# Two-stage graph network on one core: bank fills dropped, the second stage started from the message block over the cast masks, mask conversion moved ahead of the tile steps

## The reference, cut to what matters

```
h = relu(layernorm(x))                                        # setup
Wh = h @ W;  e = leaky_relu(Wh@a1 + (Wh@a2).T, 0.2)
att = softmax(where(adj > 0, e, -9e15), axis=-1)
x = x + relu(att @ Wh)                                        # first stage, attention
h = relu(layernorm(x))                                        # per tile of 128 rows
node = h @ W1                                                 # 16 columns
m = einsum('nk,nkf->nf', node, einsum('nc,kcf->nkf', h, W2))  # the "messages"
x = x + relu(adj @ m + node @ b)                              # second stage, gather
```

## Time and profile before

| | |
|---|---|
| median of 3 runs | 1854.64 us (1854.27 to 1855.09) |
| profiled execution | 1854.6 us, its span 1852.9 us |
| busy: PE / PEld | 1820.1 us (98%) / 1582.7 us (85%) |
| busy: DVE / ACT / POOL | 1206.4 (65%) / 1328.4 (72%) / 702.5 us (38%) |
| first stage, matmuls L812 | 8192 records, 979.2 us busy |
| second stage, matmuls L856 | 2048 records, 558.5 us busy |
| mean granted TensorE clock | 0.996 |

### The profile page before, as it was taken

How to read it: one execution, slowest core, us unless ns; L and a number is a source line. 1 busy time by engine, 2 the same in 40 slices (tenths; PEclk the granted TensorE clock), 3 DMA queues, 4 the chain that set the end, 5 groups by cost and what they waited for, 6 DMA issues and landing times.

```text
span 1852.9 us, 38382 instructions
## 1 busy us (share of the span) xinstructions
PE 1820.1 (98%) x13364; PEld 1582.7 (85%) x13364; DVE 1206.4 (65%) x1519; ACT 1328.4 (72%) x2145; POOL 702.5 (38%) x524
## 2 busy tenths in 40 slices
PE   8899999999999999999999999999999999999998
PEld 5799989888988988898888889888777788888886
DVE  7566667777776777777677777767655543443434
ACT  5866788778778878887887788788455655555554
POOL 0000256655655665565556556555544400000000
PEclk9999999999999999999999999999999999999999
DMA  9788876776777677767767776772843344345330
GB/s 297 294 332 319 321 285 242 297 289 265 265 301 285 243 293 291 269 259 301 287 245 294 286 275 253 295 288 110 357 154 145 145 159 182 136 174 207 149 150 23
DMA packets 105811, 452.23 MB, mean 244 GB/s; under 512 B 6736, under 2 KB 15136, under 8 KB 87968
## 3 DMA queue, kind: packets, MB, share of 16 engines
q1 hardware_dynamic: 86720, 356.53, 51.7%
q10 hardware_dynamic: 12208, 75.62, 10.0%
q0 software_dynamic: 6832, 19.41, 2.8%
HBM read 364.46 MB, written 87.07 MB: 244 GB/s over the span
## 4 chain that ended last, share of the span: by engine, by line
PE 91%; DVE 4%; ACT 2%; issue 2%; DMA 0%; DVEq 0%; SPq 0%; ACTq 0%
PE ot_ps L812 47%; PE mt_ps L856 13%; PE ot_ps L856 13%; PE hw_ps L776 11%; PE mt_ps L746 6%; PE h_ps L771 1%; DVE p_sb L903 1%; ACT wh_mask L497 1%; DVE att L960 1%; DVE p_sb L888 1%; ACT prod L574 1%; DVE p_sb L984 1%; DMA wh_mask<-in_x_dram 0%; DVE keep L965 0%; PE h_ps L783 0%
## 5 line engine op out<-in xcount | busy, mean ns | idle before, releaser
L812 PE MATMUL ot_ps<-wh_mask,p_sb 128*128 (+1 forms) x8192 | 979.2, 277 | 4.9 <-DVE p_sb L984 4.9
L812 PEld LDWEIGHTS ot_ps<-wh_mask,p_sb 128*128 128x128 f32 x8192 | 941.1, 192 | 6.6 <-issue 5.9
L984 DVE SCALAR_TENSOR_TENSOR p_sb<-zb,qcol,mt 128x1024 f32<-128x1024 uint8 (+1 forms) x512 | 770.9, 1535 | 266.7 <-ACT mt L509 213.4
L379 POOL TENSOR_TENSOR prod<-prod 128x1024 f32<-128x1024 f32 (+2 forms) x192 | 413.0, 2151 | 515.4 <-ACT prod L574 499.0
L497 ACT ACTIVATE wh_mask<-adj_sb 128x2048 uint8<-128x2048 f32 x256 | 492.6, 1928 | 1.1 <-ACT mt L509 1.1
L638 ACT ACTIVATE mask<-adj_sb 128x1024 fp32r<-128x1024 uint8 x240 | 255.3, 1065 | 176.3 <-PE ot_ps L856 176.3
L509 ACT ACTIVATE mt<-mt_ps 128x1024 uint16<-128x1024 uint16 x256 | 267.7, 1046 | 144.4 <-PE mt_ps L746 142.4
L1024 DVE CAST mask<-adj_sb 128x1024 fp32r<-128x1024 uint8 x272 | 201.9, 749 | 250.1 <-PE mt_ps L856 248.2
L574 ACT ACTIVATE prod<-hw_ps,node 128x128 f32<-128x128 f32 x1024 | 278.8, 385 | 92.1 <-PE hw_ps L776 92.1
L856 PE MATMUL mt_ps<-mask,msgs 128*128 128x512 f32 x1024 | 282.9, 398 | 4.2 <-issue 3.4
L856 PE MATMUL ot_ps<-mask,msgs 128*128 128x512 f32 x1024 | 275.6, 391 | 0.9
(11 more groups left out here) (113 smaller groups left out, 582.5 us busy)
## 6 DMA issues: line engine op xcount, KB each, us to landing
adj_sb<-in_adj_dram SPq DMA_DIRECT2D x128, 2048.0 KB, 7.9
maskT_d<-mt ACTq DMA_DIRECT2D x64, 1024.0 KB, 5.2
adj_sb<-maskT_d SPq DMA_DIRECT2D x32, 2048.0 KB, 7.7
keep_d<-keep POOLq DMA_DIRECT2D x64, 128.0 KB, 5.9
p_sb<-keep_d SPq DMA_DIRECT2D x4, 2048.0 KB, 12.0
msg_d<-msg POOLq DMA_DIRECT2D x56, 128.0 KB, 5.9
msgs<-msg_d SPq DMA_DIRECT2D x7, 1024.0 KB, 8.8
wh_mask<-in_x_dram SPq DMA_DIRECT2D x8, 512.0 KB, 7.5
```

The source lines that it names most:

```text
L379: pool.tensor_tensor(prod[:, 0:n, :], prod[:, 0:n, :], prod[:, n:2 * n, :], ALU.add)\
L812: ins = pe.matmul(ot_ps[h][:, (t - t0) * ROW:(t - t0 + 1) * ROW], p_sb[:, r, t * P:(t + 1) * P], rows, start=False, stop=end and t == t1 - 1)
L984: dve.scalar_tensor_tensor(p_sb[:, r, :], zbf[:, bass.ds((ib % 2) * BLK, BLK)], qcol[:, bass.ds(tile + b_, 1)], mtb[:, p, k, :, b_], ALU.m ...
```

## The change

Four things change, all in the order of work and in waits; no tile changes its size.

1. `start_block` is gone. The first L812 matmul of each bank in a block has `start=True` (before: the zeros matmul had), and in front of it PE waits for its bank alone (`ot_copied`). The eight transposes of the turn's first step come ahead of these waits. For this PE's first turn of a block is written out ahead of its loop (`alone=True`), as DVE's was.
2. `ORDER = (5, 0, 1, 2, 3, 4, 6, 7)`: the second stage takes j block 5 first. Its messages are loaded by SP once all transposes are done, ahead of the waits for stores and L812.
3. PE waits for the last copies of the `ot_ps` banks only at the half ib = 1 of the first step, and ACT converts its half of step 0 ahead of these copies.
4. In the first pass DVE converts step t+1 at step t, ahead of the tile steps of t (before: step t, behind them).

```
-            def start_block(ib, last):
-                for h in range(3):
-                    if not (isinstance(ib, int) and ib == 0):
-                        pe.wait_ge(ot_copied, 3 * ib - 2 + h)
-                    pe.matmul(ot_ps[h][:, :], zeros16[:, :], zeros16[:, :].unsqueeze(1).to_broadcast([P, 4, P]), start=True, stop=False)
...
+                            begin = isinstance(jg, int) and jg == 0 and p == 0 and k == 0 and b_ == 0
...
                             for h, (t0, t1) in enumerate(GROUPS):
+                                if begin and finish:
+                                    pe.sem_inc(past_pe, 1)
+                                    pe.wait_ge(ot_copied, 3 * ib - 2 + h)
+                                    pe.sem_inc(past_pe, 1)
...
-                                                    p_sb[:, r, t * P:(t + 1) * P], rows, start=False, stop=end and t == t1 - 1)
+                                                    p_sb[:, r, t * P:(t + 1) * P], rows, start=begin and t == t0, stop=end and t == t1 - 1)
...
-            attention_loop(pe, turn, start_block)
+            attention_loop(pe, turn, alone=True)
```

```
+        ORDER = (5, 0, 1, 2, 3, 4, 6, 7)
...
             sp.wait_ge(turned, C * NB * NB)
+            sp.wait_ge(kept, (ORDER[0] + 1) * T + 2)
+            load_messages(0)
             for p in range(2):
                 sp.wait_ge(mt_stored[p], 16 * NB * IT)
             for r in range(4):
                 sp.wait_ge(p_used[r], 4 * NB * IT)
-            for s in range(NB - 1):
-                sp.wait_ge(kept, (s + 1) * T + 2)
+            for s in range(1, NB - 1):
+                sp.wait_ge(kept, (ORDER[s] + 1) * T + 2)
                 load_messages(s)
```

```
                         if ends_block(jg) and p == 1 and k == 3:
+                            if last:
+                                convert(0, True, 0)
                             copy_sums(ib)
...
-            for t in range(2):
-                convert(0, True, t)
+            convert(0, True, 1)
```

```
                     for ib in range(2):
+                        if t == 0 and first and ib == 1:
+                            pe.wait_ge(ot_copied, 3 * NB)
...
-            pe.wait_ge(ot_copied, 3 * NB)
             pe.wait_ge(evicted, C * NB * NB)
```

```
             for t in range(NT):
                 mi, at = t // PERIOD, t % PERIOD
+                if 2 <= t + 1 < NT:
+                    convert(0, True, t + 1)
                 if at == 1 and mi < T:
                     finish_last(mi, (2,))
                 elif at == PERIOD - 1 and mi + 1 < T:
                     finish_last(mi + 1, (0, 1))
-                if t >= 2:
-                    convert(0, True, t)
```

More of the change, by code:

```diff
@@ L306, in load_messages @@
             def load_messages(s):
-                sp.dma_start(msgs[:, s * T:(s + 1) * T, :, :].rearrange("p n c f -> p (n c f)").bitcast(FP32),
-                             msg_d[:, s * T:(s + 1) * T, :].rearrange("p n f -> p (n f)").bitcast(FP32))\
+                o = ORDER[s]
+                sp.dma_start(msgs[:, o * T:(o + 1) * T, :, :].rearrange("p n c f -> p (n c f)").bitcast(FP32),
+                             msg_d[:, o * T:(o + 1) * T, :].rearrange("p n f -> p (n f)").bitcast(FP32))\
                   .then_inc(msgs_in[s], 16)
@@ L323, in load_masks @@
                 sp.dma_start(masks_w[:, q, :, :],
-                             maskT_d[s, bass.ds(2 * ii, 2), :, :].rearrange("i p w -> p i w"))\
+                             maskT_d[ORDER[s], bass.ds(2 * ii, 2), :, :].rearrange("i p w -> p i w"))\
                   .then_inc(masks_in[q], 16)
@@ L592, in copy_sums, with convert @@
                                    ot_ps[h][:, 0:(t1 - t0) * ROW], ACT.Copy).then_inc(ot_copied, 1)
+            def convert(ii, first, t):
+                s, r = t // T, t % 2
+                for ib in range(2):
+                    if not on_dve(first, t, ib):
+                        act.wait_ge(masks_in[s % 4], 16 * (ii * (NB // 4) + s // 4 + 1))
+                        if not (first and t < 2):
+                            act.wait_ge(conv_used[r][ib], ii * (NT // 2) + t // 2)
+                        act.activation(mask32[:, r, ib, :], masks[:, s % 4, ib, t % T // 2, :, t % 2], ACT.Copy)\
+                           .then_inc(conv_act, 1)
             def turn(i, ib, jg, finish, last):
@@ L629, in _ @@
             attention_loop(act, turn)
[L631 to L639, removed]
             def take_bank(ii, ib):
@@ L855, in gather @@
                             for h in range(2):
-                                ins = pe.matmul(acc_ps[2 * ib + h][:, :], msgs[:, t, c, :],
+                                ins = pe.matmul(acc_ps[2 * ib + h][:, :], msgs[:, ORDER[s] * T + t % T, c, :],
                                                 mask32[:, r, ib, h * HB:(h + 1) * HB],
```

## The result

| | before | changed |
|---|---|---|
| median | 1854.67 us (4 runs) | 1897.2 us (1895.03 to 1899.43, 4 runs) |
| ratio, 95% interval | | 1.0231 [1.0217, 1.0245] |
| profiled execution / span | 1854.6 / 1852.9 us | 1895.03 / 1893.4 us |
| last L812 (now L816) starts | 1329.67 us | 1336.86 us |
| first matmul of the second stage | 1335.02 us | 1338.29 us |

The kernel is 42.5 us slower. I had forecast 1878 us in a range of 1858 to 1888: the sign and the deciding place were right, the size was not. Already the table has a surprise: of the 40.4 us between the profiled executions 7.2 arose in the first stage, where I had forecast a small gain. (Of the 29 runs of the kernel before that stand beside e3, e8, e9 and e10 further down, one took 1876.46 us at a mean clock of 0.946; it doesn't move the medians, but it may move the ratios and intervals given there.)

What follows compares the result with a forecast made beforehand. PE, busy 98% of the span, was taken to bound the kernel. Terms -0.9 (fills), -4.3 (between stages), +22.4 (DVE's order) and +6 (clock) sum to +23.2 us on 1854.6: 1878 us, range 1858 to 1888.

Steps and rivals of the forecast that it cites:

- the deciding place: First pass of the second stage: DVE's moved tile steps meet POOL's adds and stall PE seven times, +22.4 us.
- The fills (change 1): First term, first stage: dropping zero matmuls gains only at the change into block 1, -0.9 us; bounds 0 and -5.2.
- PE's seams into that code show no gap: PE's written-out first turn of a block: costed at nothing; 2 us were it 0.3 us each time.
- Between the stages (changes 2 and 3): Start of second stage: message wait -3.45, half clock -1.7, late `xn` +0.85; sum -4.3 us.
- `xn` late: First tile of the second stage: `xn` held by POOL's add to about 1336.0, PE wants it at 1335.2; cost 0.85 us.
- DVE's order (change 4): First pass, tiles 1 to 7: PE stalls 3.6 us each (3.1 to 4.0), less 0.4 us that goes; +22.4 us.
- the 0.4 us that I let go in each period: First pass: short PE stalls of 0.4 us per period of seven steps, expected to vanish with the new order.
- the 4.0 us that I had worked out for that case: First pass: upper bound of PE's stall if L955, L960 and L965 are each held by one of POOL's adds.
- The clock: Behind the seven stalls: half of seven falls to half clock, 1.7 us each; +6 us, bounds 0 and 12.

Runs made afterwards that it cites:

- e3: Kernel before with changes 2 and 3 alone (zero fills and DVE's order as before): 1851.5 us, ratio 0.9977.
- e8: Changed kernel plus 14 unread matmuls of zeros in each of PE's seven idle times of the first pass: 1883.1 us, ratio 1.0144.
- e9: As e3, but DVE converts step t+1 at step t, behind the tile steps for mean and variance and ahead of `xn`: 1853.8 us, ratio 0.9986.
- e10: As e9, but `xn` too stands ahead of the conversion of step t+1: 1851.5 us, ratio 0.9975.
- e2: Changed kernel with change 1 alone undone (zero fills back, PE's first turn not written out): 1887.3 us, ratio 1.0178.
- e1: Changed kernel with change 4 alone undone (DVE converts step t behind the tile steps of t): 1859.9 us, ratio 1.0026.
- e5: Kernel before with PE's first turn of every block written out ahead of its loop, zero fills and waits kept: 1867.2 us, ratio 1.0069.
- e6: As e1, but PE's last turn of a block is inside the loop (two turns of code), with three closing matmuls of zeros: 1867.2 us, ratio 1.0071.
- e7: Changed kernel with POOL's three large adds cut to 16 columns for tiles 1 to 7 of the last block: 1862.5 us, ratio 1.0043.
- e4: Kernel before with change 4 alone (DVE converts step t+1 ahead of the tile steps of t): 1891.1 us, ratio 1.0192.

## Why the prediction was wrong, point by point

**The fills (change 1): the step that failed.** I gave -0.9 us; it is +9.9 us (changed kernel against e2), or +8.4 (e1 against e3). The reasoning on the fills held: at the change into block 1 the 0.9 us are gained, and at the last change of blocks, where PE goes on without a way back, it waits 0.37 us for weights with fills (e2) and 0.92 us without them, so what the fills took goes into the wait. What failed is the sentence "I cost it at nothing, since PE's seams into that code show no gap; were it 0.3 us each time, 2 us". The seams that I looked at belong to code passed once; the new turn lies inside the loop over blocks, and makes its body three turns instead of two. e5 shows that this alone costs 12.3 us, the stretches of the instruction queue that packets come again in every round, and e6 that with a body of two turns they don't. Per way back 2.6 to 3.0 us, five times, of which the fills and the wait for weights gave back a part, and a fall of the clock in some executions on top.

The packets go with the length of the loop: 87 in the changed kernel, e1, e5 and e7 and 88 in e8, which have three turns in it, 31 or 32 in all the others, which have two. In the kernel before, the loop brings in 6 packets in its first round and none in the five behind it. In the changed kernel it is 10 in each of the four rounds between its five ways back (3 of them within 10 us around the way back, as 356 to 366, and 7 behind, as 366 to 520). I take from it that two turns stayed loaded and three did not; no run here measured where between them the limit lies. That the queue was silent while the loop ran stood in the trace of the kernel before; it was the first thing to look at ahead of writing out a turn, and I had not looked.

**Between the stages (changes 2 and 3).** Forecast -4.3 us, measured -3.3 (e3). The steps held: the first message block was there in time, no half clock, `xn` late by 0.46 us (e3: 0.38) where I had 0.85; up to the first transpose e3 gains 4.65 us. What I missed is the period behind it, 1.67 us longer, with a second late conversion and one in step 7.

**DVE's order (change 4).** Mechanism and place held, and the size nearly: a stall of 3.79 us each time, where I had taken 3.6 between 3.1 and 4.0. L960 (before: L955), which had no row, is held like the others (2.49 us). e7 shows that POOL's adds do it, e4 that the edit needs no other. Of the 0.4 us that I let go in each period at most half went: a stall of 3.79 us adds 3.6 us to its period (e8), so this term is 25 us, not 22.4. All three steps were held, for 2.49, 1.25 and 0.83 us; the 4.0 us that I had worked out for that case, my upper bound, is as far above the measured 3.79 as my middle value is below it.

**The clock.** I counted half of seven falls, 6 us, and bounded them by 12. All seven idle times were followed by half clock, two of them for twice as long, and e8 prices them at 14.1 us. (By e4, 36.1 less 25 for the stalls, it is 11; that profile has one long fall.) The two rows that I had (3.33 and 3.35 us of idle time, both followed by a fall) spoke for all seven; I discounted them because they were few, and my upper bound took each fall to last as long as the one in the earlier trace rows.

By edits the sum closes: -3.3 (e3) + 36.1 (e4) + 9.9 (changed kernel against e2) = +42.7 us against +42.5 measured. My sum had +23.2. Of the 19 us that are missing 10.8 lie in the first term, 7.7 in DVE's order and the clock together (36.1 against 22.4 + 6), and 1.0 between the stages. With the first term alone put right the sum would still be only just above the range (1889 us, against a measured 1897); with DVE's order and the clock alone put right it would be 1886.

## What to carry to other kernels

Before a turn is written out ahead of a loop, count the code of the outer loop around it and look at the instruction queue while the loop runs: here it was silent from 365 to 1160 us with two turns in the loop, and with three it moved 46 packets there and PE stood idle for 2.5 to 3.1 us at each way back. A step of VectorE that is moved by two places may land beside GpSimd's long adds, which here made a step of 0.35 us last 2.49; look at what runs there, not only at whether its result is needed later. And an idle time of 3.3 to 3.8 us on TensorE is to be charged with the half clock behind it: here it followed both in the kernel before (3.33 and 3.35 us) and all seven of 3.79 us in the changed kernel, where it cost some 2 us each (14.1 us over seven, e8).

## What the runs showed of the hardware that I had not expected

- The instruction queue moved 31 or 32 packets with two turns in PE's loop over blocks, 87 or 88 with three, and with three PE stood idle for 2.5 to 3.1 us at each way back; from 365 to 1160 us it was 46 packets in the changed kernel and none in the kernel before.
- In the changed kernel the half clock behind an idle time of 3.79 us lasted some 6.8 us twice, 3.4 us five times.
- Shorter idle times were followed by half clock too, some of them: of the 25 at the way back (2.5 to 3.1 us; changed kernel, e1, e5, e7, e8) 7 were, of the seven of 3.79 us in the changed kernel all.
- Matmuls whose result nobody reads, put into the seven idle times, made the kernel 14.1 us faster (e8: 1883.1 us against 1897.2).
- Beside the three large adds of 1024, 512 and 256 columns three VectorE steps of 128 columns lasted 2.49, 1.25 and 0.83 us, one beside each; beside adds of 16 columns, issued at the same place, they lasted 0.35, 0.29 and 0.29 (e7).
